# Sorting six sequences' rows by expert through DRAM in a one-core language model tower with 64 experts

## The chip, the cores and the metric

One core of a Trainium2 chip runs the whole computation in one launch. The metric is device microseconds, the median of several executions. Its five engines work in order, each through its own queue, and wait for one another on semaphores: TensorE (PE; its weight loads are PEld), VectorE (DVE), ScalarE (ACT), GpSimd (POOL) and SyncE (SP), which issues most DMAs.

## What is computed

Eight sequences of 512 tokens pass three parts. All data are fp32, D = 128.

```
e  = fine_embed[ids] ++ softmax(cluster_logits[ids] + b) @ coarse          # gather of 128 values per token
xn = rms_norm(layer_norm(e)); scores = xn qk xn^T * decay mask             # q, k, v, o folded into qk and vo
x2 = x1 + mem_mul * (scores @ xn vo)                                       # with a carried state per tile
h2 = e + x2 + op_mul * gelu(rms_norm(x2) @ read_mix + bias) @ write_w
x3 = layer_norm(h2)
p  = softmax(x3 @ router_w + b); the 6 largest of 64, normalised, are the gates
out = h2 + mean of 2 shared experts(x3) + sum over chosen experts: gate * (silu(x3 Wg) * (x3 Wu)) Wd
```

An expert has hidden size F = 64, and takes at most 768 tokens over all sequences, in token order; later ones are dropped.

## The kernel before, in words

Experts are taken in pairs, so that 2 x 64 hidden values fill 128 partitions: 32 routed pairs and one shared pair, `PAIRS` = 33. Every token goes through every pair, and the gate, zero where the expert was not chosen, is multiplied into the hidden values. Matrix products of the experts use fp32r (faster, less exact) three times each, on high and low parts: `gate_up` (L456 to L458) makes six products of 512 columns per pair, `down` (L443 to L445) three more, which lag by `LAG` = 4 pairs. Per pair ACT computes silu (L580) and copies the high part (L587), DVE multiplies by the up product (L828) and subtracts for the low part (L835), and POOL multiplies by the gate rows (L985). SP fetches those rows from `gates_dram`, broadcast over 64 partitions each (L278), into a ring of four.

The work of a sequence before its experts (call it the front part: embedding, attention, norms, router, gates) is written as steps placed at pair numbers by the tables `DVE_AT`, `PE_AT`, `ACT_AT`, `POOL_AT`. While sequence b runs its 33 pairs, the late steps of b + 1 and the early ones of b + 2 are issued in between, so one sequence's front part is spread over one to two sequences of pairs. Sequence 0's front part, and the split of the expert weights into high and low parts (ACT L614, DVE and POOL L257), run before the first pair. The token limit is kept by a running count (`taken`, L775, carried in `taken_end`), and the gates go to DRAM (L294).

## Time and profile before

| | |
|---|---|
| median of 3 runs | 775.56 us (775.4 to 778.88) |
| span of the profiled execution | 776.1 us, 0.5 us above that median |
| PE busy | 685.0 us, 88% |
| DVE busy | 636.5 us, 82% |
| POOL busy | 523.6 us, 67% |
| ACT busy | 430.9 us, 56% |
| moved by DMA | 80.20 MB, in 48862 packets |

The profile's times are those of one execution. Matmul records overlap, so the distance between two starts says what one costs, not its own length. "Idle before" names what ended the idle time in front of a group.

### The profile page before, as it was taken

To read this page: it belongs to the slowest core of one execution; us is meant where nothing else is said; L and a number is where in the kernel's file an instruction comes from. 1 tells how busy PE (TensorE), PEld (TensorE's weight loads), DVE (VectorE), ACT (ScalarE), POOL (GpSimd) and SP (SyncE) were. 2 spreads that over 40 slices of the span, in tenths; PEclk is the share of its full clock that TensorE was granted. 3 is DMA by queue.
4 is the path that set the end of the run, shared out by engine and by line. 5 is a ranking of instruction groups with operands and counts; after the bars stand their busy time and mean duration, and the time that the engine had idled before them with its cause. 6 is when DMAs were issued, how large, how long until landed. Compare 5 with 4: busy or idle time off the path is not lost.

```text
span 776.1 us, 11821 instructions
## 1 busy us (share of the span) xinstructions
PE 685.0 (88%) x3079; PEld 534.7 (69%) x3079; DVE 636.5 (82%) x1207; ACT 430.9 (56%) x745; POOL 523.6 (67%) x353
## 2 busy tenths in 40 slices
PE   4245899998998989997999989989899999999997
PEld 3234678766786677766777667867677688768885
DVE  4866778797898889898798988989888987897665
ACT  4333376643855557644666448555566456655553
POOL 5421667766676767767577677767677668768775
PEclk9976899998999999999999999999999999999999
DMA  5400423333333233224233333233333334425431
GB/s 210 156 31 0 129 86 106 107 95 93 94 101 112 91 99 122 97 77 123 81 115 102 96 92 114 98 108 99 98 110 98 93 115 121 118 78 144 139 128 58
DMA packets 48862, 80.20 MB, mean 103 GB/s; under 512 B 9504, under 2 KB 13728, under 8 KB 48800
## 3 DMA queue, kind: packets, MB, share of 16 engines
q1 hardware_dynamic: 47776, 77.44, 31.4%
q0 software_dynamic: 1024, 2.10, 1.2%
q8 instruction: 19, 0.31, 0.2%
q14 instruction: 43, 0.35, 0.1%
HBM read 76.35 MB, written 3.15 MB: 102 GB/s over the span
## 4 chain that ended last, share of the span: by engine, by line
DVE 25%; POOL 25%; issue 23%; PE 18%; ACT 3%; DMA 1%; POOLq 1%; SPq 1%; DVEq 0%; ACTq 0%
POOL hid L985 20%; DVE hid_lo L835 6%; DVE hid L828 5%; PE bank_u L456 2%; DVE xn L693 2%; PE bank_u L458 1%; PE bank_u L457 1%; POOL inv L966 1%; PE bank_g L456 1%; DVE turns L762 1%; PE bank_g L458 1%; PE bank_g L457 1%; PE bank_y L443 1%; PE bank_y L444 1%; PE bank_y L445 1%
## 5 line engine op out<-in xcount | busy, mean ns | idle before, releaser
L985 POOL TENSOR_TENSOR hid<-hid,gate_rows 128x512 f32<-128x512 f32 x256 | 412.8, 1623 | 177.7 <-DVE hid L828 174.5
L580 ACT ACTIVATE hid<-bank_g 128x512 f32<-128x512 f32 x264 | 157.6, 597 | 165.1 <-PE bank_g L458 159.8
L835 DVE TENSOR_TENSOR hid_lo<-hid,hid_hi 128x512 fp32r<-128x512 f32 x264 | 231.7, 878 | 17.7 <-ACT hid_hi L587 17.5
L828 DVE TENSOR_TENSOR hid<-hid,bank_u 128x512 f32<-128x512 f32 x264 | 179.0, 679 | 69.4 <-ACT hid L580 39.0
L587 ACT ACTIVATE hid_hi<-hid 128x512 fp32r<-128x512 f32 x264 | 165.9, 628 | 91.0 <-POOL hid L985 83.2
L456 PE MATMUL bank_g<-x_hi,gate_hi 128*128 128x512 f32 x264 | 115.7, 438 | 6.7 <-ACT hid L580 6.7
L456 PE MATMUL bank_u<-x_hi,up_hi 128*128 128x512 f32 x264 | 108.9, 412 | 3.0 <-DVE hid L828 2.7
L443 PE MATMUL bank_y<-hid_hi,down_hi 128*128 128x512 f32 x264 | 105.6, 400 | 3.1 <-ACT hid_hi L587 3.0
L457 PE MATMUL bank_g<-x_hi,gate_lo 128*128 128x512 f32 x264 | 105.7, 400 | 0.0
L444 PE MATMUL bank_y<-hid_hi,down_lo 128*128 128x512 f32 x264 | 105.6, 400 | 0.0
L458 PE MATMUL bank_g<-x_lo,gate_hi 128*128 128x512 f32 x264 | 105.4, 399 | 0.0
L458 PE MATMUL bank_u<-x_lo,up_hi 128*128 128x512 f32 x264 | 105.3, 399 | 0.0
L457 PE MATMUL bank_u<-x_hi,up_lo 128*128 128x512 f32 x264 | 105.2, 399 | 0.0
L445 PE MATMUL bank_y<-hid_lo,down_hi 128*128 128x512 f32 x264 | 104.9, 397 | 0.0
L456 PEld LDWEIGHTS bank_u<-x_hi,up_hi 128*128 128x128 f32 x264 | 50.5, 191 | 26.3 <-DVE hid L828 15.7
L443 PEld LDWEIGHTS bank_y<-hid_hi,down_hi 128*128 128x128 f32 x264 | 49.9, 189 | 20.6 <-ACT hid_hi L587 5.5
L456 PEld LDWEIGHTS bank_g<-x_hi,gate_hi 128*128 128x128 f32 x264 | 50.5, 191 | 19.6 <-ACT hid L580 9.6
L458 PEld LDWEIGHTS bank_u<-x_lo,up_hi 128*128 128x128 f32 x264 | 50.3, 191 | 12.2
L458 PEld LDWEIGHTS bank_g<-x_lo,gate_hi 128*128 128x128 f32 x264 | 50.4, 191 | 12.0
L445 PEld LDWEIGHTS bank_y<-hid_lo,down_hi 128*128 128x128 f32 x264 | 50.0, 189 | 12.1
L457 PEld LDWEIGHTS bank_u<-x_hi,up_lo 128*128 128x128 f32 x264 | 50.5, 191 | 10.2
L457 PEld LDWEIGHTS bank_g<-x_hi,gate_lo 128*128 128x128 f32 x264 | 50.6, 192 | 9.4 <-issue 1.7
(197 smaller groups left out, 836.9 us busy)
## 6 DMA issues: line engine op xcount, KB each, us to landing
gate_rows<-gates_dram SPq DMA_DIRECT2D x512, 128.0 KB, 2.9
hid<-gate_t_dram SPq DMA_DIRECT2D x3, 704.0 KB, 4.1
out_dram<-later SPq DMA_DIRECT2D x8, 256.0 KB, 3.0
gate_rows<-up_t_dram SPq DMA_DIRECT2D x2, 704.0 KB, 4.8
hid<-down_t_dram SPq DMA_DIRECT2D x2, 704.0 KB, 4.7
gates_dram<-gates_t SPq DMA_DIRECT2D x8, 128.0 KB, 2.3
later<-up_t_dram SPq DMA_DIRECT2D x1, 704.0 KB, 8.4
later<-down_t_dram SPq DMA_DIRECT2D x1, 704.0 KB, 6.2
```

What stands on the lines that cost most here:

```text
L443: pe.matmul(y[:, :], w_hi["down"][:, p, :], hid_hi[:, s, :], start=(p == 0), stop=False)
L444: pe.matmul(y[:, :], w_lo["down"][:, p, :], hid_hi[:, s, :], start=False, stop=False)
L445: pe.matmul(y[:, :], w_hi["down"][:, p, :], hid_lo[:, s, :], start=False, stop=(p == PAIRS - 1)).then_inc(sem("down_done"), 1)
L456: pe.matmul(o, w_hi[name][:, p, :], x3_hi[par][:, :], start=True, stop=False)
L457: pe.matmul(o, w_lo[name][:, p, :], x3_hi[par][:, :], start=False, stop=False)
L458: pe.matmul(o, w_hi[name][:, p, :], x3_lo[par][:, :], start=False, stop=True).then_inc(sem("pe_" + name), 1)
L580: act.activation(hid[:, slot(par, p), :], bank_g[(p + par) % 2][:, :], ACT.Silu).then_inc(sem("silu"), 1)
L587: act.activation(hid_hi[:, s, :], hid[:, s, :], ACT.Copy).then_inc(sem("hid_hi"), 1)
L693: last = dve.tensor_scalar(xn2[:, t, :], x2[:, t, :], inv2[:, t:t + 1], None, ALU.mult)
L828: dve.tensor_tensor(hid[:, s, :], hid[:, s, :], bank_u[(p + par) % 2][:, :], ALU.mult)\
L835: dve.tensor_tensor(hid_lo[:, s, :], hid[:, s, :], hid_hi[:, s, :].bitcast(F32), ALU.subtract)\
L985: pool.tensor_tensor(hid[:, s, :], hid[:, s, :], gate_rows[:, row, :], ALU.mult)\
```

## The change

Sequences 0 and 7 (`DENSE`) are treated as before: all 33 pairs, in place, but with one fp32 product where there were three fp32r ones, one PSUM bank each for gate (`bank_x`) and up (`bank_g`), and both multiplications on DVE. The other six (`SPARSE`) form two passes of three. In each:

- The running count starts at the expert's first row of a DRAM array `x_rows` (a stretch of 3200 rows per expert). `slots` holds, for each token, the rows of its six experts: the eight largest of a key per expert. POOL then scatters each tile of 128 tokens six times, each row holding the 128 values of x3 and the 64 gates (768 bytes).
- From the counts, `dve_lists` and `pe_lists` make a list of 136 tiles of 128 rows, each of one expert: offsets into the weights, gate column and DRAM row. The number is a fixed bound: 64 + (9216 - 64) / 128 = 135, rounded up to 34 steps of four tiles (`QUADS`), whatever the router does. A part of the list can be repeats.
- Each of the 34 steps loads four tiles (SP), transposes them, multiplies by gate and up weights side by side (128 columns), silu, times gate and up (DVE, 64 columns a tile), transposes, multiplies by the down weights, and ACT stores the four results to `y_rows`. The offsets are read from `lists` into registers, on SP, DVE and (twice) on PE.
- After a pass POOL fetches every token's six result rows (`y_slots`), and DVE sums them and adds them to h2.

The order is now written in half steps h, from -31 to 287, for all engines. A front part has 30 half steps; those of the eight sequences start at `START`. Sequence 0's pairs run from h = 0, two half steps each; pass one from h = 70, pass two from 138, sequence 7's pairs from 212. The shared experts of the six are computed apart (`shared_in`, `shared_out`). The norm's `hx` sum moves from POOL to DVE.

```diff
-CHUNKS = [(n, p0) for p0 in range(0, PAIRS, CHUNK) for n in ("gate", "up")] + \
-    [("down", p0) for p0 in range(0, PAIRS, CHUNK)]
+DENSE = (0, 7)
+PASSES = ((1, 2, 3), (4, 5, 6))
...
+ROW = D + EXPERTS
+ZEROS = P
+STRETCH = ZEROS + len(SPARSE) * SEQ
...
+START = (-30, -16, 0, 16, 32, 54, 76, 98)
+D_AT = {0: 0, 7: 212}
+E_AT = 70
+DOWN_LAG = 2
+LOAD_AHEAD = 6
...
+SCATTER_AT, SCATTERS_PER_HALF = 26, 1.5
+FETCH_AT = {0: E_AT + 2 * QUADS + 8, 1: E_AT + 2 * E_STEPS + 8}
+FETCHES_PER_HALF = 1.4
+COMBINE_LAG = 4
...
+        def sp_tiles(sp, g):
...
+            if g >= XT_RING:
+                sp.wait_ge(sem("hid"), g - XT_RING + 1)
+                sp.wait_ge(sem("pe_xt"), g - XT_RING + 1)
+            _, at = nc.values_load_multi_w_load_instructions(
+                lists[q][0:1, j, 3 * QUAD:4 * QUAD], engines=(ENG.SP,), min_val=0, max_val=EXPERTS * STRETCH - P)
+            for t in range(QUAD):
+                sp.dma_start(xt[:, g % XT_RING, t, :], x_rows[bass.ds(at[t], P), :])\
+                  .then_inc(sem(f"xt{g % XT_RING}"), 16)
...
-        def gate_up(pe, b, par, p):
...
-            for name, banks, freed in (("gate", bank_g, "silu"), ("up", bank_u, "up_used")):
-
-                wait(pe, freed, q - 1)
-                o = banks[ring][:, :]
-                pe.matmul(o, w_hi[name][:, p, :], x3_hi[par][:, :], start=True, stop=False)
-                pe.matmul(o, w_lo[name][:, p, :], x3_hi[par][:, :], start=False, stop=False)
-                pe.matmul(o, w_hi[name][:, p, :], x3_lo[par][:, :], start=False,
-                          stop=True).then_inc(sem("pe_" + name), 1)
+        def pe_dense(pe, d, b, p, half):
...
+                if p:
+                    pe.wait_ge(sem("silu"), q)
+                pe.matmul(bank_x[:, :], w_in[:, 0, p * P:p * P + P], x3_t(b)[:, :], start=True, stop=True)\
+                  .then_inc(sem("pe_gate"), 1)
+                if p:
+                    pe.wait_ge(sem("up_used"), q)
+                pe.matmul(bank_g[:, :], w_in[:, 1, p * P:p * P + P], x3_t(b)[:, :], start=True, stop=True)\
+                  .then_inc(sem("pe_up"), 1)
...
+        def pe_gate_up(pe, g):
+            q, j = divmod(g, QUADS)
+            _, at = nc.values_load_multi_w_load_instructions(
+                lists[q][0:1, j, 0:QUAD], engines=(ENG.PE,), min_val=P, max_val=P + (EXPERTS - 1) * F)
+            pe.wait_ge(sem("xT"), g + 1)
+            if g == 0:
+                pe.wait_ge(sem("up_used"), PAIRS)
+            else:
+                pe.wait_ge(sem("hid"), g)
+            for t in range(QUAD):
+                last = pe.matmul(bank_g[:, t * P:t * P + P], xT[:, g % 2, t * P:t * P + P], w_in[:, :, bass.ds(at[t], F)],
+                                 start=True, stop=True, skip_group_check=True)
+            last.then_inc(sem("pe_gu"), 1)
...
+        def dve_rows(dve, g):
+            q, j = divmod(g, QUADS)
+            _, at = nc.values_load_multi_w_load_instructions(
+                lists[q][0:1, j, 2 * QUAD:3 * QUAD], engines=(ENG.DVE,), min_val=D, max_val=ROW - 1)
+            dve.wait_ge(sem("sg"), g + 1)
+            wait(dve, "pe_hT", g - 1)
+            for t in range(QUAD):
+                last = dve.scalar_tensor_tensor(hid[:, g % 2, t * F:(t + 1) * F], sg[:, t, :],
+                                                xt[:, g % XT_RING, t, bass.ds(at[t], 1)], tiles(bank_g)[:, t, F:],
+                                                ALU.mult, ALU.mult)
+            last.then_inc(sem("hid"), 1)
+
+        def dve_combine(dve, m):
+            i, t = divmod(m, TILES)
+            b = SPARSE[i]
+            dve.wait_ge(sem(f"yg{m % YG_RING}"), 16 * TOP * (m // YG_RING + 1))
+            dve.tensor_reduce(ysum[:, m % 2, :], yg[:, m % YG_RING, :].rearrange("p (k d) -> p d k", d=D), AX.X, ALU.add)\
+               .then_inc(sem("y_sum"), 1)
...
+            dve.tensor_tensor(h2[b][:, t, :], h2[b][:, t, :], ysum[:, m % 2, :], ALU.add).then_inc(sem("combined"), 1)
...
+        def scatter(pool, b, i):
+            t, k = divmod(i, TOP)
...
+            pool.indirect_dma_start(x_rows[:, :],
+                                    bass.IndirectOffsetOnAxis(ap=slots[b][:, t * 8 + k:t * 8 + k + 1], axis=0),
+                                    xg[b % 2][:, t, :], None).then_inc(sem(f"scattered{b % 2}"), 16)
+
+        def fetch(pool, q, i):
...
+            if i == 0:
+                for r in range(Y_RING):
+                    pool.wait_ge(sem(f"y_stored{r}"), quad_rows(r, QUADS * (q + 1)))
...
+            if k == 0:
+                wait(pool, "y_sum", m - YG_RING + 1)
+            pool.indirect_dma_start(yg[:, m % YG_RING, k * D:(k + 1) * D], None, y_rows[q][:, :],
+                                    bass.IndirectOffsetOnAxis(ap=y_slots[b][:, t * 8 + k:t * 8 + k + 1], axis=0))\
+                .then_inc(sem(f"yg{m % YG_RING}"), 16)
```

In the order of instructions the change stands as follows. First PE's experts in place: one pair, before (PE's queue in the loop over sequences).

```order
L456 MATMUL bank_g<-x_hi,gate_hi 128x512
L457 MATMUL bank_g<-x_hi,gate_lo 128x512
L458 MATMUL bank_g<-x_lo,gate_hi 128x512
L456 MATMUL bank_u<-x_hi,up_hi 128x512
L457 MATMUL bank_u<-x_hi,up_lo 128x512
L458 MATMUL bank_u<-x_lo,up_hi 128x512
L443 MATMUL bank_y<-hid_hi,down_hi 128x512
L444 MATMUL bank_y<-hid_hi,down_lo 128x512
L445 MATMUL bank_y<-hid_lo,down_hi 128x512
```

The same engine with the change, at about pair 30 of sequence 0, beside the end of sequence 4's front part and the beginning of sequence 5's: L535, L539 and L548 are gate, up and down, the rest are front steps.

```order
L535 MATMUL bank_x<-x_t_dense,w_in 128x512
L539 MATMUL bank_g<-x_t_dense,w_in 128x512
L488 MATMUL bank_f<-w_dn,shared_hid 128x128 x4
L407 MATMUL bank_f<-xn_hi,qk_hi 128x512
L408 MATMUL bank_f<-xn_hi,qk_lo 128x512
L409 MATMUL bank_f<-xn_lo,qk_hi 128x512
L548 MATMUL bank_y<-y_sb,w_dn 128x512
```

Nine products per pair became three, and there is a group of front products between nearly all of them. Next the sparse steps on DVE, inside pass two: `bank_h` holds transposed hidden rows, L1053 is the product with silu and gate.

```order
L1174 COPY hT<-bank_h 64x256
L1048 TENSOR_LOAD lists
L1048 ISA x8
L1053 ISA
L1053 SCALAR_TENSOR_TENSOR hid<-sg,xt,bank_g 128x64
```

The last two rows come four times in a step. The kernel before has no load of registers on DVE; it stands here behind the copy of the step before. PE, in the same steps (L565 transposes the rows in, L578 is gate and up, L587 transposes the hidden rows):

```order
L565 MATMUL bank_x<-ident,xt 128x128 x4
L570 TENSOR_LOAD lists
L570 ISA x8
L578 ISA
L578 MATMUL bank_g<-w_in,xT 128x128
```
```order
L587 MATMUL bank_h<-ident,hid 128x128 x2
L592 TENSOR_LOAD lists
L592 ISA x8
L602 ISA
L602 MATMUL bank_y<-w_d,hT 128x128
```

Each of the two products comes four times behind its own load. Last POOL, while sequence 1 to 3 are scattered and, at the end of its queue, the fetches of both passes.

```order
L1195 DMA x_rows<-xg,slots 204800x192 x6
L1231 TENSOR_TENSOR inv<-var,neg_half 128x4
L1195 DMA x_rows<-xg,slots 204800x192 x4
L1220 TENSOR_TENSOR inv<-var,neg_half 128x8
L1195 DMA x_rows<-xg,slots 204800x192 x9
```
```order
L1195 DMA x_rows<-xg,slots 204800x192 x4
L1212 DMA yg<-y_rows,y_slots 128x128 x144
```

Where one gate product stood per pair (L985), POOL now issues indirect DMAs, with the powers of the norms between them.

## Rows read from the trace of the kernel before

**Rows 1.** The page, parts 1 and 4: busy time of each engine; chain by engine.
```profile
PE 685.0 (88%) x3079; PEld 534.7 (69%) x3079; DVE 636.5 (82%) x1207; ACT 430.9 (56%) x745; POOL 523.6 (67%) x353
...
DVE 25%; POOL 25%; issue 23%; PE 18%; ACT 3%; DMA 1%; POOLq 1%; SPq 1%; DVEq 0%; ACTq 0%
```

**Rows 2.** Stretches of the span; the columns are in the first line.
```profile
core 0: us, PE busy (x) PEld busy (x) DVE busy (x) ACT busy (x) POOL busy (x), PEclk, DMA share, GB/s
...
10.00:77.00 67.00, 30.57 (x114) 23.09 (x112) 48.45 (x116) 24.70 (x35) 21.99 (x13) 0.84 0.28 101
...
164.00:251.00 87.00, 80.12 (x359) 62.42 (x360) 72.66 (x140) 50.42 (x88) 60.32 (x41) 0.96 0.32 102
...
338.00:776.00 438.00, 409.60 (x1861) 320.08 (x1861) 364.63 (x656) 251.06 (x440) 313.02 (x203) 1.00 0.34 105
```

**Rows 3.** Groups by form: busy us, mean ns, idle before and releasers.
```profile
L985 POOL TENSOR_TENSOR hid<-hid,gate_rows 128x512 f32<-128x512 f32 x256 | 412.8, 1623 | 177.7 <-DVE hid L828 174.5 <-DMA gate_rows<-gates_dram 2.5
L835 DVE TENSOR_TENSOR hid_lo<-hid,hid_hi 128x512 fp32r<-128x512 f32 x264 | 231.7, 878 | 17.7 <-ACT hid_hi L587 17.5
L828 DVE TENSOR_TENSOR hid<-hid,bank_u 128x512 f32<-128x512 f32 x264 | 179.0, 679 | 69.4 <-ACT hid L580 39.0 <-PE bank_u L458 29.5
...
L580 ACT ACTIVATE hid<-bank_g 128x512 f32<-128x512 f32 x264 | 157.6, 597 | 165.1 <-PE bank_g L458 159.8 <-DVE hid_lo L835 2.1 <-issue 0.6
...
L682 DVE SCALAR_TENSOR_TENSOR turns<-turns,decay_cols,bank_f 128x128 f32<-128x128 f32 x16 | 5.6, 348 | 0.6
```

**Rows 4.** Timeline of PE: start us, us, instruction; one pair to the next.
```profile
310.64 0.39 PE L456 MATMUL bank_g<-x_hi,gate_hi 128*128 128x512 f32 x1
...
312.74 0.40 PE L456 MATMUL bank_g<-x_hi,gate_hi 128*128 128x512 f32 x1
```

**Rows 5.** Timeline of PE at three places: fp32 products and transposes.
```profile
297.19 1.02 PE L387 MATMUL bank_f<-xn_t,read_mix 128*128 128x512 f32 x2
...
298.28 0.39 PE L457 MATMUL bank_g<-x_hi,gate_lo 128*128 128x512 f32 x1
...
215.82 1.05 PE L393 MATMUL bank_f<-write_w,vals 128*128 128x128 f32 x8
216.63 0.48 PE L456 MATMUL bank_g<-x_hi,gate_hi 128*128 128x512 f32 x1
...
314.84 0.65 PE L399 MATMUL bank_f<-ident,xn 128*128 128x128 f32 x4
```

**Rows 6.** Timeline of DVE in the first sequence's front part.
```profile
22.57 3.90 DVE L644 TENSOR_SCALAR xn<-emb,mv,inv 128x128 f32<-128x128 f32 x4
...
26.39 1.61 DVE L257 TENSOR_TENSOR up_lo<-gate_rows,up_hi 128x1408 fp32r<-128x1408 f32 x1
...
33.65 4.03 DVE L650 TENSOR_SCALAR x<-emb,mv,inv 128x128 f32<-128x128 f32 x4
...
48.59 4.78 DVE L693 TENSOR_SCALAR xn<-shared,inv 128x128 f32<-128x128 f32 x4 [1.31 <-POOL inv L955]
...
63.02 1.12 DVE L716 TENSOR_SCALAR xn<-h,mv,inv 128x128 f32<-128x128 f32 x4 [0.80 <-POOL inv L961]
```

**Rows 7.** Timeline of POOL: two gathers.
```profile
4.86 0.94 POOL L945 DMA_INDIRECT emb<-table_dram,idx  x1 [0.30 <-issue]
...
6.11 0.94 POOL L945 DMA_INDIRECT emb<-table_dram,idx  x1 [0.30 <-issue]
```

**Rows 8.** Gate-row issues of SP (ns min/median/max), landing, and POOL's DMA queue.
```profile
L278 SPq DMA_DIRECT2D gate_rows<-gates_dram x512: 465/468/1425, 79.2 to 761.1; - x171
L278 SPq MOVE gate_rows<-gates_dram x256: 29/29/38, 165.7 to 521.4; - x128
L278 SPq FUSED_REGOPS  x254: 37/37/42, 165.7 to 521.3; - x127
...
q0 software_dynamic: 1024, 2.10, 1.2%
...
gate_rows<-gates_dram SPq DMA_DIRECT2D x512, 128.0 KB, 2.9
```

More of the change, by code:

```diff
@@ L43 @@
 SENTINEL = 2.0
-RING = 6
-GATE_RING = 4
-LAG = 4
-SPLIT_LAG = 2
-GATHER_AT = (1, 2, 3, 4)
-DVE_AT = dict(xn=0, xn_lo=2, x1=5, xn_dec=5, y_lo=4, scores=6, state=6, x2=8, result=10, logits=9, xn2=11, exp_sum=12,
-              h=15, bn1=16, h2=17, bn3=17, mv1=18, x3=19, x3_lo=21, router=24, prob=26, top=27, chosen=28, gates=29,
-              taken=31)
-PE_AT = dict(xn_t=1, y=3, z_scores=5, state=6, mem=7, out=8, exp_t=11, xn2_t=12, vals=13, coarse=14, op=16, x3_t=20,
-             router=23, gates_t=30)
@@ new lines @@
+TILE_BOUND = EXPERTS + (ROWS_OF_PASS - EXPERTS) // P
+QUADS = (TILE_BOUND + QUAD - 1) // QUAD
+LIST = QUADS * QUAD
+MAX_TILES = len(PASSES[0]) * SEQ // P
+XT_RING, Y_RING, YG_RING = 4, 3, 3
+GATE_RING, HID_RING = 3, 3
+START = (-30, -16, 0, 16, 32, 54, 76, 98)
[3 more added lines that the diff above has]
+LOAD_AHEAD = 6
+E_STEPS = len(PASSES) * QUADS
+H_FIRST, H_LAST = START[0] - 1, D_AT[7] + 2 * (PAIRS + DOWN_LAG) + 6
+DVE_AT = dict(logits=0, exp_sum=2, h=3, xn=5, xn_lo=6, xn_dec=6, x1=7, y_lo=7, scores=8, state=9, x2=10, hx=11, xn2=13,
+              h2=16, x3=18, router=20, prob=22, chosen=23, taken=24, slots=25, shared_up=27, shared_add=29)
@@ L542, in act_late @@
                 act.wait_ge(sem("pe_z_scores"), b + 1)
[L543 to L547 removed]
+                for j in range(2):
+                    act.activation(z[:, 2 * j:2 * j + 2, :], z_scores(par, j)[:, :, 0, :], ACT.Copy).then_inc(sem("z"), 1)
@@ L838, in dve_out @@
[L838 to L856 removed]
+            if k == DVE_AT["taken"]:
+                dve_taken(dve, b, f1)
@@ new lines, in _ @@
+                for d, b in enumerate(DENSE):
+                    if h == D_AT[b] + 2 * (PAIRS + DOWN_LAG) + 2:
+                        dve.wait_ge(sem("pe_out"), d + 1)
+                        dve.tensor_tensor(h2[b][:, :, :], tiles(bank_y), h2[b][:, :, :], ALU.add).then_inc(sem("result"), 1)
+                now = step_e(h)
+                if now:
+                    s, half = now
+                    if half == 0 and 0 <= s - 2 < E_STEPS:
+                        g = s - 2
+                        dve.wait_ge(sem("pe_hT"), g + 1)
+                        wait(dve, "pe_ey", g - 1)
+                        dve.tensor_copy(hT[:, g % 2, 1, :], bank_h[F:, 0:2 * P]).then_inc(sem("hT_odd"), 1)
+                    if half == 0 and 0 <= s - 1 < E_STEPS:
+                        dve_rows(dve, s - 1)
```

1302 lines of the change are left out of this document (759 added, 543 removed).

## The prediction

> **What bounds the kernel now.** I read the engines' totals first, then busy time by stretch, the costliest groups, and last the order of single matmuls. PE is busy for 88% of the span and DVE for 82%, while the chain that ended last is spread over DVE, POOL, issue and PE [rows 1]. The stretches say more [rows 2]: 67 us (10 to 77) go to the first sequence's front part, with PE busy for 31 us only; from there every sequence takes 87 us, with PE busy for 80 and DVE for 73. So after 77 us TensorE sets the pace. One expert pair is nine fp32r products of 512 columns; the gate product of one pair starts at 310.64 and that of the next at 312.74, so a pair costs 2.10 us [rows 4], and 33 pairs 69 of the 87 us. The reader should see that ScalarE, POOL and the gate-row transfers have slack, and that DVE has little.
>
> **What the change removes.** All eight sequences now pay 33 pairs; afterwards two do. Also gone: the weight splits, the hi/lo splits of hidden rows (264 x 0.88 us of DVE), and POOL's gate product (256 x 1.62 us) [rows 3]. POOL's arithmetic also held DVE up: three groups of four small DVE operations took 3.90, 4.03 and 4.78 us in the first front where another such group took 1.12 [rows 6].
>
> **Prices.** An fp32 product of 512 columns: the two records begin at 297.19, and the product after the next starts at 298.28; less the 0.23 us (2.10 / 9) of the product between, that is 0.86 us [rows 5]. An fp32 product of 128 columns: eight records (four products) from 215.82 to the next start at 216.63, 0.20 each [rows 5]. Four transposes take 0.65 us at most, about 0.4 in a stream [rows 5]. A dense pair is thus 3 x 0.86 = 2.6 us of PE where it was 2.1: one fp32 product costs more than two fp32r ones but less than four. On DVE it is two products of 0.68, 1.36 us [rows 3]; the old second operation's 0.88 included waits for POOL. A front part costs DVE 72.7 - 33 x (0.68 + 0.88) = 21 us [rows 2, 3]; with the slot keys, the second gate pass and the shared expert's two operations I take 24 for a sorted sequence. It costs PE 80.1 - 69.3 = 11, with the new products 13. As a chain it took 67 us (10 to 77); less the 9.3 us above what three normal groups need, and five weight splits of 1.6 us [rows 6], some 49 us, over 25 of the new half steps: 2.0 us each.
>
> **Unseen prices.** The register load (one from `lists` per sparse step on DVE and on SP, two on PE) appears nowhere. Its lower end is a register operation's 0.03 to 0.04 us, since a register could fill as fast as it is moved; its upper end is a whole DMA round trip, 2.9 us from issue to landing [rows 8]. I take 1.2 us, nearest to a POOL indirect issue of 0.94 to 1.25, which also makes a sequencer fetch and compute [rows 7]. For eight bounds checks and four address operations I take 0.4 us at 0.03 to 0.04 each [rows 8]. The gate product of 64 columns on DVE (four per step): below the 0.35 us of the 128-column form from PSUM [rows 3], above nothing; 0.25. Scatter and fetch: the gathers start 1.25 us apart (4.86, 6.11) [rows 7], and I take that for all 288 new ones. [...]
>
> **Stage by stage** (half steps h of the new order).
> A, until h = 0. Ten us of loading, 14 halves with one front at 2.0, 16 with two at 2.5: 10 + 28 + 40 = **78 us**. Before, this stage ended at 77 [rows 2]. Dropping the weight splits is eaten by letting front 1 run through its 17th step first.
> B, h 0 to 70: first sequence dense, fronts 2 to 5 beside it. DVE: 3.9 fronts x 24 + 5 for the tile lists + 33 x 1.36 = 144 us, 2.1 per half; PE: 33 x 2.6 + 3.9 x 13 = 136. Neither the floors nor the 2.0 chain can all be met, because every engine is in order and heavy steps meet: with fronts 16 halves apart, layer norm meets the new logits, top-8 meets xn_lo, the gates meet y_lo, and the counts meet the scores. These four halves hold about 18.5 us of DVE; the other twelve go at the chain's 2.0. (18.5 + 24)/16 = 2.7. 70 x 2.7 = **189 us**. POOL's 72 scatters (90 us) lie beside this.
> C, pass one, 34 steps, fronts 5 (second half), 6 and 7 beside. A sparse step is a loop: PE gate/up of step s (4 x 0.20), its hidden transposes and signal (0.4), DVE copy (0.35), DVE register load and checks (1.6), four products (1.0), then gate/up of s + 1: 4.15 us. DVE holds 2.95 of that. The fronts add 72/34 = 2.1 to the same in-order queue, 5.05 in all, and fill most of the hole; I add 0.45 for waits: 34 x 5.5 = **187 us**.
> D, pass two, no front left after a few steps. The loop alone, 4.15, raised to 4.5 because PE's sequencer has two loads with checks (3.2) and some 50 matrix instructions to send in the same time: 34 x 4.5 = **153 us**. The first pass's fetches (72 x 1.25 = 90) and sums lie in DVE's hole.
> E, drain of three steps, **9 us**, then the last sequence dense. Alone it would be 33 x 2.6 + 8 = 94. But the 72 fetches of pass two start only now, need 90 us on POOL, and DVE waits in order for each fourth of them: 94 us with landing until the last sum, which stands at half 56 of the dense stage; 14 halves at 1.3 remain, then 8 us of tail. **120 us**.
> Sum: 78 + 189 + 187 + 153 + 9 + 120 = **736 us**, against the profiled execution's own span of 776.1, which is 0.5 above the median of the runs, 775.56; I leave it uncorrected. In short, eight stages of 87 us, bound by PE arithmetic, turn into about 660 us bound by DVE and by sequencer latency. The arithmetic shrinks far more than the time does.
>
> **The clock.** [...] A pure sparse step keeps PE busy for 2.3 of 4.5 us, 51%. I charge nothing: the mean of 0.84 would add 0.15 us to the gate/up part, 10 us in all. [...]
>
> **Rivals.**
> R1, faster, 630 us. The queues overlap better than I think: halves in B at DVE's own 2.2 (154), C at 4.9 (167), D at 3.6 because loads overlap the hidden transposes (122), fetches not held up by a slow start, E at 100: 78 + 154 + 167 + 122 + 9 + 100. For it: from 164 to 251 PE is busy for 92% of the stretch although the same fronts run beside it [rows 2]. Against: there a front had 33 pairs of slack, now 8.
> R2, slower, 811 us. The register load on DVE sits inside the loop of every sparse step. At 2.3 us it adds 1.1 x 68 = 75 us. It decides from (776 - 736)/68 = 0.6 us more, that is from 1.8 us per load. For: a DMA round trip is 2.9 us; against: nothing has to be written and signalled.
> R3, slower, 796 us. DMA becomes the bound. In D a step moves 393 KB of tiles, 262 KB of results and 180 KB of fetches, 186 GB/s, where 105 GB/s took a share of 0.34 [rows 2]: 0.60 at the same price. If rows of 512 to 768 bytes cost double, a step needs 5.4 us, +0.9 x 68. Against: the gathers' 4096 rows of 512 bytes took 1.2% of sixteen engines' span, 36 ns each [rows 8].
> R4: B and C go worse, 3.2 per half and 6.5 per step, 805 us.
>
> **How the numbers follow.** Forecast 0.48, R1 0.18, R2 0.20, R3 0.07, R4 0.07. About 0.5% (4 us) is what a measurement of this kernel can tell from no change. The forecast's own range, 690 to 790, has 0.38 below 772; with R1 and a little of R2 to R4 faster has 0.57, same 0.06, slower 0.37. The range 640 to 850 leaves out half of R1 and the far ends of R2 to R4. Since both signs are likely, the likeliest case's own range matters: 690 to 790.
>
> **What would show it.** Right: DVE between a hidden-row copy and the next one spends about 1.2 us in which nothing is busy (the load); pure sparse steps 4.5 us apart; first dense stage 175 to 205 us long with PE under 75% busy; POOL issues spaced 1.25 us and DVE waiting for `yg` in the last stage. Wrong: sparse steps under 3.8 or above 5.3 us, tiles arriving after PE asks for them (waits of PE for `xt`), a granted clock near 0.5 through pass two, or a front that takes far more than 16 halves' time. Gates or slots cannot shorten the work: 34 steps per pass run whatever the router picks.

## The result, and the profile after

The changed kernel takes 823.57 us (median of 4 runs, 821.62 to 824.75) against 776.96 (775.40 to 778.88) for the kernel before, a ratio of 1.0587 with a 95% interval of 1.0549 to 1.0625: 6% slower, where 736 us and 5% faster was forecast. The profiled execution has a span of 823.0 us.

The page of the changed kernel: totals, granted clock in 40 slices, chain, and the groups that carry the new work (line, engine, operation, names | busy us, mean ns | idle before them and its releasers).

```profile
PE 615.1 (75%) x2709; PEld 424.9 (52%) x2709; DVE 427.3 (52%) x1308; ACT 280.5 (34%) x543; POOL 354.7 (43%) x361
...
PEclk9999799899999968668667987989897866899898
...
PE 43%; DVE 21%; POOL 13%; issue 13%; DVEq 4%; ACT 3%; DMA 1%; POOLq 0%; SPq 0%; ACTq 0%
...
L1212 POOL DMA_INDIRECT yg<-y_rows,y_slots x144 | 139.9, 972 | 191.4 <-DMA y_rows<-y_sb 128.5
...
L578 PE MATMUL bank_g<-w_in,xT 128*128 x544 | 104.2, 352 | 33.3 <-DVE hid L1053 19.0
L602 PE MATMUL bank_y<-w_d,hT 64*128 x544 | 95.9, 327 | 34.8 <-DVE hT L1174 26.6
...
L1053 DVE SCALAR_TENSOR_TENSOR hid<-sg,xt,bank_g 128x64 f32<-128x64 f32 x272 | 58.6, 275 | 86.7 <-issue 86.5
L1174 DVE COPY hT<-bank_h 64x256 f32<-64x256 f32 x68 | 29.0, 426 | 123.7 <-PE bank_h L587 123.0
```

Against the same parts of before [rows 1], every engine lost work (DVE 636.5 to 427.3 us, PE 685.0 to 615.1), and none is near its limit: the time went into waits between engines. DVE stood idle 86.7 us ahead of L1053, the gating of the rows, with nothing named but "issue" (1.27 us a step, over 68 steps), and 123.7 us ahead of L1174 for PE's transposes, while PE waited for both of these. Two engines that wait for each other are a loop, not a bottleneck.

The span by stage. The bounds are starts of PE instructions: the first dense product (L535, 88.1), the row transposes (L565) of step 0 (283.7), of step 27, the first with no front part beside it (489.4), of step 34 (pass two, 523.9) and of the last, step 67 (685.6).

```profile
core 0: us, PE busy (x) PEld busy (x) DVE busy (x) ACT busy (x) POOL busy (x), PEclk, DMA share, GB/s
0.00:88.10 88.10, 47.01 (x171) 36.34 (x172) 41.64 (x153) 20.08 (x43) 19.72 (x28) 0.96 0.62 196
88.10:283.70 195.60, 157.60 (x609) 85.66 (x609) 146.47 (x450) 78.89 (x137) 123.04 (x116) 0.97 0.29 96
283.70:489.40 205.70, 146.54 (x795) 123.58 (x792) 98.82 (x376) 80.97 (x158) 72.04 (x73) 0.74 0.37 108
489.40:523.90 34.50, 27.26 (x156) 22.78 (x155) 9.21 (x37) 13.18 (x28) 0.00 (x0) 0.80 0.46 131
523.90:685.60 161.70, 125.49 (x727) 104.98 (x726) 63.12 (x193) 61.61 (x132) 68.65 (x72) 0.83 0.62 169
685.60:823.00 137.40, 111.21 (x261) 51.58 (x260) 68.04 (x103) 25.74 (x45) 71.26 (x72) 0.87 0.42 115
```

| stage | forecast | measured |
|---|---|---|
| A, until the first dense product | 78 | 88 |
| B, sequence 0 dense, fronts 2 to 5 | 189 | 196 |
| C, pass one (34 steps) | 187 | 240 |
| D, drain and E, pass two to the end | 282 | 299 |

Of the 87 us that the forecast lacks, 53 lie in C, and there in its first 27 steps: 7.6 us each where 5.5 was forecast. The last seven took 4.9 each, and the 33 steps from 34 to 67 also 4.9, against a forecast of 4.5.

One such step on the timeline (start us, us, instruction [idle before <-releaser]), here at full clock:

```profile
649.98 0.85 DVE L1053 SCALAR_TENSOR_TENSOR hid<-sg,xt,bank_g 128x64 f32<-128x64 f32 x4 [1.27 <-issue]
...
651.10 1.15 PE L578 MATMUL bank_g<-w_in,xT 128*128 x8 [0.55 <-DVE hid L1053]
...
652.09 0.38 PE L587 MATMUL bank_h<-ident,hid 128*128 128x128 f32 x2
...
652.51 0.42 DVE L1174 COPY hT<-bank_h 64x256 f32<-64x256 f32 x1 [1.68 <-PE bank_h L587]
...
653.50 1.15 PE L602 MATMUL bank_y<-w_d,hT 64*128 x8 [1.03 <-DVE hT L1174]
...
654.21 0.86 DVE L1053 SCALAR_TENSOR_TENSOR hid<-sg,xt,bank_g 128x64 f32<-128x64 f32 x4 [1.27 <-issue]
```

This is the loop that the forecast described: gating, gate and up products, hidden transposes, copy, load, next gating: 4.23 us from 649.98 to 654.21 (forecast 4.15). The steps alone take longer than this loop, 4.64 on average in the 19 of them in which the granted clock was 1.00; the first question below shows that most of the rest is PE's own queue. What the 1.27 and 1.03 us hold, the two sequencers show (ns min/median/max):

```profile
L570 PEldq FUSED_REGOPS  x272: 146/148/165, 285.7 to 690.2; - x136
L570 PEldq SEQ_ASSERT  x272: 18/18/24, 285.9 to 690.5; - x136
L570 PEldq TENSOR_LOAD <-lists x68: 327/333/594, 285.1 to 689.0; - x68
...
L1048 DVEq FUSED_REGOPS  x272: 183/186/211, 291.6 to 695.1; - x136
L1048 DVEq SEQ_ASSERT  x272: 23/23/41, 291.9 to 695.3; - x136
L1048 DVEq TENSOR_LOAD <-lists x68: 339/342/598, 291.0 to 693.9; - x68
```

A load of four words takes 0.33 to 0.34 us. The range check that goes with every word is the pair FUSED_REGOPS and SEQ_ASSERT of these lines; it takes 0.166 us on PE (148 + 18 ns) and 0.209 on DVE, so the four cost 0.66 and 0.84, two thirds of the whole: 1.0 us on PE, twice a step, 1.18 on DVE.

### The profile page after: what moved, and what is told of

Its sections match the earlier page's. It is cut to its first block, busy times and chain, and to the rows that moved or that the text cites. A ratio compares the mean times of both kernels' runs of the same rounds, so it can differ in the third digit from the quotient of the medians.

```text
span 823.0 us, 13195 instructions
## 1 busy us (share of the span) xinstructions
PE 615.1 (75%) x2709; PEld 424.9 (52%) x2709; DVE 427.3 (52%) x1308; ACT 280.5 (34%) x543; POOL 354.7 (43%) x361
## 3 DMA queue, kind: packets, MB, share of 16 engines
q0 software_dynamic: 12544, 25.71, 10.7%
## 4 chain that ended last, share of the span: by engine, by line
PE 43%; DVE 21%; POOL 13%; issue 13%; DVEq 4%; ACT 3%; DMA 1%; POOLq 0%; SPq 0%; ACTq 0%
PE bank_g L578 11%; POOL yg L1212 8%; PE bank_y L602 6%; PE bank_x L565 4%; DVEq L1048 4%; POOL x_rows L1195 3%; DVE hid L1053 2%; DVE hT L1174 2%; PE bank_h L587 2%; PE bank_x L535 2%; PE bank_g L539 2%; PE bank_f L432 2%; PE bank_y L548 1%; PE bank_f L396 1%; PE bank_f L435 1%
## 5 line engine op out<-in xcount | busy, mean ns | idle before, releaser
L1212 POOL DMA_INDIRECT yg<-y_rows,y_slots x144 | 139.9, 972 | 191.4 <-DMA y_rows<-y_sb 128.5
L1195 POOL DMA_INDIRECT x_rows<-xg,slots x144 | 145.7, 1012 | 65.8 <-issue 41.7
L578 PE MATMUL bank_g<-w_in,xT 128*128 x544 | 104.2, 352 | 33.3 <-DVE hid L1053 19.0
L602 PE MATMUL bank_y<-w_d,hT 64*128 x544 | 95.9, 327 | 34.8 <-DVE hT L1174 26.6
L578 PEld LDWEIGHTS bank_g<-w_in,xT 128*128 128x128 f32 x544 | 91.7, 255 | 46.2 <-issue 46.1
L602 PEld LDWEIGHTS bank_y<-w_d,hT 64*128 64x128 f32 x544 | 81.2, 226 | 52.8 <-issue 52.8
L1053 DVE SCALAR_TENSOR_TENSOR hid<-sg,xt,bank_g 128x64 f32<-128x64 f32 x272 | 58.6, 275 | 86.7 <-issue 86.5
L1174 DVE COPY hT<-bank_h 64x256 f32<-64x256 f32 x68 | 29.0, 426 | 123.7 <-PE bank_h L587 123.0
L539 PE MATMUL bank_g<-x_t_dense,w_in 128*128 128x512 f32 x132 | 71.9, 627 | 17.0 <-DVE xt L1151 17.0
L535 PE MATMUL bank_x<-x_t_dense,w_in 128*128 128x512 f32 x132 | 74.7, 650 | 0.0
L539 PEld LDWEIGHTS bank_g<-x_t_dense,w_in 128*128 128x128 f32 x132 | 26.5, 207 | 56.1 <-issue 29.7
L565 PE MATMUL bank_x<-ident,xt 128*128 128x128 f32 x272 | 54.2, 333 | 0.3 <-ACT xT L761 0.3
L766 ACT ACTIVATE sg<-bank_g 128x256 f32<-128x256 f32 x68 | 26.1, 383 | 83.0 <-PE bank_g L578 82.9
L749 ACT ACTIVATE xt<-bank_x 128x512 f32<-128x512 f32 x33 | 19.7, 597 | 90.9 <-PE bank_x L535 84.4
L565 PEld LDWEIGHTS bank_x<-ident,xt 128*128 128x128 f32 x272 | 37.3, 169 | 8.1 <-issue 3.5
L548 PE MATMUL bank_y<-xt,w_dn 128*128 128x512 f32 x66 | 36.3, 638 | 0.0
```

What stands on the lines that cost most here:

```text
L535: pe.matmul(bank_x[:, :], w_in[:, 0, p * P:p * P + P], x3_t(b)[:, :], start=True, stop=True)\
L539: pe.matmul(bank_g[:, :], w_in[:, 1, p * P:p * P + P], x3_t(b)[:, :], start=True, stop=True)\
L548: pe.matmul(bank_y[:, :], w_dn[:, p, :], hid_d[b][:, p % HID_RING, :], start=(p == 0), stop=(p == PAIRS - 1)).then_inc(sem("down_done"), 1)
L565: last = pe.transpose(bank_x[:, t * P:t * P + P], xt[:, r, t, 0:D], ident[:, :])
L578: last = pe.matmul(bank_g[:, t * P:t * P + P], xT[:, g % 2, t * P:t * P + P], w_in[:, :, bass.ds(at[t], F)], start=True, stop=True, skip_g ...
L602: last = pe.matmul(bank_y[:, t * P:t * P + P], hT[:, g % 2, t % 2, (t // 2) * P:(t // 2 + 1) * P], w_d64[:, bass.ds(at[t], P)], start=True ...
```

## The experiments

Times of the kernel before, beside these runs, had medians of 777.29 to 778.42 us; the ratios are to those. For each kernel I read the same three stretches as above: steps 0 to 27 (beside fronts), 27 to 67 (alone), and from step 67 to the end. These stretches are those of one profiled execution each, and differences of a few us between them mean little: the last one took 137.4 us in the changed kernel and 132.4 to 135.4 in five kernels whose edits hardly touch that stage (e1, e2, e3, e5, e13).

| kernel | median us | ratio, 95% interval | 0-27 | 27-67 | rest |
|---|---|---|---|---|---|
| changed | 823.57 | 1.0549 to 1.0625 | 205.7 | 196.3 | 137.4 |
| e1_pe_nocheck | 801.39 | 1.0262 to 1.0315 | 191.3 | 195.5 | 133.6 |
| e2_dve_nocheck | 786.04 | 1.0080 to 1.0135 | 176.8 | 188.9 | 132.4 |
| e3_dve_load_first | 788.80 | 1.0117 to 1.0151 | 181.3 | 191.5 | 133.8 |
| e4_both | 708.95 | 0.9072 to 0.9128 | 159.9 | 135.5 | 127.0 |
| e9_nocheck_all | 709.50 | 0.9089 to 0.9178 | 160.8 | 134.4 | 128.7 |
| e6_filler | 819.30 | 1.0511 to 1.0549 | 204.0 | 194.6 | 132.9 |
| e8_both_filler | 730.38 | 0.9347 to 0.9418 | 168.2 | 146.1 | 129.1 |
| e10_one_load | 710.92 | 0.9104 to 0.9231 | 158.5 | 135.3 | 126.5 |
| e5_late_rows | 898.17 | 1.1513 to 1.1598 | 138.4 | 201.9 | 135.4 |
| e13_copy_later | 781.94 | 1.0037 to 1.0084 | 170.1 | 190.3 | 132.4 |
| e14_copy_later_nocheck | 698.82 | 0.8968 to 0.9067 | 146.3 | 134.0 | 128.5 |
| e16_swap_later_nocheck | 788.84 | 1.0118 to 1.0183 | 234.8 | 140.5 | 129.4 |
| e7_no_fetch | 801.52 | 1.0247 to 1.0334 | 207.0 | 199.3 | 111.5 |
| e11_rate | 693.55 | 0.8886 to 0.8970 | 159.8 | 132.2 | 114.2 |
| e12_best | 699.51 | 0.8932 to 0.9029 | 160.1 | 136.3 | 114.1 |
| e15_all | 688.35 | 0.8815 to 0.8888 | 149.9 | 137.2 | 114.7 |
| e17_checks_kept | 769.60 | 0.9875 to 0.9912 | 170.5 | 189.8 | 119.7 |

**First question: what do load and checks cost, and on which engine?** Theory T1: PE's queue is the loop. T2: the loop runs through DVE. The range checks are left out with an argument of the load call; the computation is the same.

```diff
 e1, at both of PE's loads; e2, at DVE's load
-  ..., min_val=..., max_val=...)
+  ..., min_val=..., max_val=..., skip_runtime_bounds_check_because="...")
 e3 (e4: this, and no checks on PE, DVE and SP)
+                    at = dve_load(s - 1) if half == 0 and 0 <= s - 1 < E_STEPS else None
                     if half == 0 and 0 <= s - 2 < E_STEPS:
                         g = s - 2
                         dve.wait_ge(sem("pe_hT"), g + 1)
```

> The four range checks behind each of PE's two register loads per sparse step are left out; nothing else changes. Theory T1 (PE's own queue is the loop of a sparse step: rows in, load, gate/up, hidden transposes, load, down; 4.6 us at full clock): a step without fronts falls from 4.6 to about 4.15, where the loop through DVE takes over, and the time by 30 to 45 us, to about 785. Theory T2 (the loop runs through DVE's copy, load and four products, as the prediction had it): no change, 823 within 5.

> The four range checks behind DVE's register load are left out, 0.6 us of DVE's queue per sparse step. T1 (PE's queue is the loop): within 8 us of the changed kernel's 823. T2 (the loop through DVE): 0.6 x 68 = 41 us less, 782.

> DVE's register load and checks stand before its wait for the hidden transposes instead of behind it, so 1.3 us leave the loop through DVE (copy, load, products) and fall into its idle time. T1: within 10 us of 823. T2: 1.3 x 68 = 88 us less, 735.

> No range checks on PE, DVE and SP, and DVE's load first. T1: PE's queue becomes 4.6 - 1.3 = 3.3 us at full clock and DVE's loop 2.5, so the step without fronts goes to 3.4 to 3.8 and the time falls by 68 x 1.0 or more, to 730 to 755. T2: as e3, 735, with e1 unchanged. If the clock falls because PE's work gets no denser, less.

Neither theory holds alone, and 709 lies below every forecast for e4. Each single edit gains 22 to 38 us, about three quarters of it beside the fronts; steps alone hardly move (4.91 to 4.89, 4.72 and 4.79 us). Both together gain 115, of which 61 in the steps alone: 3.39 us each. What PE waited for ahead of its two products changes hands, and goes only when both queues are short. In order: e1, e2, e4.

```profile
L578 PE MATMUL bank_g<-w_in,xT 128*128 x544 | 106.0, 357 | 45.3 <-DVE hid L1053 42.3 <-ACT xT L761 2.8 <-issue 0.3
L602 PE MATMUL bank_y<-w_d,hT 64*128 x544 | 96.9, 330 | 1.1 <-ACT y_sb L778 0.9 <-issue 0.2
```

```profile
L578 PE MATMUL bank_g<-w_in,xT 128*128 x544 | 106.1, 357 | 19.9 <-issue 12.4 <-ACT xT L761 6.3 <-DVE hid L1053 0.8
L602 PE MATMUL bank_y<-w_d,hT 64*128 x544 | 98.7, 334 | 28.8 <-DVE hT L1174 23.9 <-ACT hT L772 3.1 <-ACT y_sb L778 0.9
```

```profile
L578 PE MATMUL bank_g<-w_in,xT 128*128 x544 | 84.7, 304 | 6.5 <-DVE hid L1055 5.5 <-issue 0.9
L602 PE MATMUL bank_y<-w_d,hT 64*128 x544 | 81.9, 293 | 4.3 <-issue 1.7 <-ACT y_sb L778 1.1 <-ACT hT L772 0.5
```

With PE's checks gone (e1), all of the wait is for DVE's gating; with DVE's gone (e2), it is "issue" and the wait for the copy, behind which PE's own second load and checks stand. So a step has two rounds of similar length, one on each queue, and the longer one counts.

That is not all that kept the single edits small in the steps alone. The granted clock over steps 27 to 67 fell too: 0.82 in the changed kernel, 0.76, 0.76 and 0.75 in e1, e2 and e3, 0.94 in e4. At the same clock more is seen. Six steps in a row at full clock (33 to 38) and two at a granted clock of 0.54 (63, 64) in the changed kernel, and six at full clock (45 to 50) in e1, in the columns of the windows above:

```profile
518.96:546.93 27.97, 18.66 (x133) 15.14 (x132) 8.07 (x32) 10.98 (x24) 1.69 (x2) 1.00 0.52 145
663.83:674.85 11.02, 10.47 (x46) 8.90 (x45) 4.09 (x13) 3.90 (x8) 0.00 (x0) 0.54 0.46 129
```

```profile
566.39:592.45 26.06, 18.48 (x133) 15.13 (x132) 11.05 (x34) 11.60 (x25) 15.41 (x18) 1.00 0.74 198
```

At full clock a step took 4.66 us, and 4.34 without PE's checks, on the way to the 4.15 to 4.23 of DVE's loop, as T1 has it; with the clock at 0.54 it took 5.51, and PE was busy for 95% of it, so there PE's own work set the pace. The lower clock of e1 hides in its mean what the shorter queue had given.

To see whether the place of DVE's load matters at all once it is short, e9 drops the checks everywhere and leaves the load where it was:

> No range checks on any queue, but DVE's register load back in its place between the copy of the transposed hidden rows and the gating (the kernel of 708.95 us has it ahead). Single edits gave -22 (PE's checks), -37 (DVE's checks), -35 (DVE's load ahead), together -115. Theory T3 (two queues take turns as the bound: a step costs the longer of PE's round and DVE's round, so either edit on DVE alone stops at PE's round of 4.5 us and PE's alone at DVE's): without checks DVE's load is 0.35 us, PE's products bound the step at 3.1 anyway, so only 0 to 0.35 x 68 us is lost: 709 to 733. Rival (moving the load is worth 35 us whatever the checks cost, since it takes the load off the way from PE to DVE to PE): 744.

709.5 us, the same as e4: T3 holds, and the rival falls. The checks alone are worth 114 us. (SP's are among them in e4 and e9 and have no run of their own; in the changed kernel PE never waited for the tiles that SP loads, so they were hardly on its path.) e10 takes one load of eight words on PE in place of two of four (`lists[q][0:1, j, 0:2 * QUAD]`, the down offsets kept until two steps later):

> The kernel of 708.95 us with one register load of eight words on PE in each step in place of two of four. In its trace PE idles 0.15 us (issue) ahead of the gate and up products and 0.35 to 0.37 us (issue) ahead of the down products in a step of 3.09. Theory L1 (a load costs 0.33 us whatever it brings in): 68 x 0.35 = 24 us less, 685. Theory L2 (it costs by the register, 0.08 us each): the time is the same, 709, and the idle moves ahead of the gate and up products.

No gain (710.92, in four runs from 707.14 to 718.03, against 708.95). The load of eight took 0.59 us at the median where four took 0.33, so most of it goes by the word (0.065 us each and some 0.07 once). L2 is right about the time; the idle time ahead of the down products went from 4.3 to 1.1 us as L1 has it, and the wait for DVE's gating rose from 5.5 to 8.6. PE's round is not all that is left of the step. The steps at full clock show the place of DVE's load too: 3.36 us on average in e9 (all 40), where it stands inside the loop, and 3.17 in e4 (35 of 40), whose other five, in which the clock fell, took 4.9.

**Second question: is it the clock?** It was 0.74 beside the fronts and 0.83 in pass two (0.82 over steps 27 to 67), lower than the 0.96 to 1.00 of the dense stages before [rows 2]. Two extra products per step keep PE at work during its waits:

```diff
+        def filler(pe, bank):
+            pe.matmul(bank[:, 0:2 * P], ident[:, :], w_in[:, 0, 0:2 * P], start=True, stop=True, skip_group_check=True)
...
             wait(pe, "hT_odd", g)
+            filler(pe, bank_h)
+            pe.wait_ge(sem("hid"), g + 1)
...
+            filler(pe, bank_y)
             pe.wait_ge(sem("hT_even"), g + 1)
```

> The changed kernel with two extra fp32 products of 256 columns in every step of rows, into a bank that is overwritten afterwards: one ahead of the wait for the gated hidden rows, one behind PE's second register load ahead of the wait for the transposed hidden rows. They read nothing that the fronts or steps write. Theory C (the granted clock, 0.73 to 0.76 in the stretches 283 to 386, 386 to 491 and 600 to 704, is a price of its own): the fillers lie in idle time and raise it; steps alone go from 4.9 to 4.5 (45 steps, -18), the steps beside fronts lose up to a quarter of the 150 us that PE is busy in 283 to 494, of which half is on the path (-18): 785 to 795. Theory Q (the steps wait in the queues for register loads, checks and for each other, and the clock only follows): no change where the fillers hide, 820 to 826, and up to 68 x 0.86 = 58 us more where they don't, 880.

> The kernel without range checks and with DVE's load ahead of its wait (708.95 us), with the same two fillers in each step. There a step alone takes 3.0 us at a granted clock of 1.00 in a stretch of 460 to 494 us, and PE is busy 33.3 of 34 us, so it has no idle time for the fillers; beside fronts the clock is 0.83 to 0.84. Theory C (clock a price of its own beside fronts): at best 12 us less there, and 45 steps x 0.86 x (1.0 to 0.5 hidden) = 20 to 39 more in the steps alone: 717 to 735. Theory Q: 747 if all fillers stand on the path.

The fillers did raise the clock (third from the end in the columns of the windows above):

```profile
285.30:489.40 204.10, 155.51 (x893) 126.24 (x891) 99.78 (x380) 82.19 (x158) 71.85 (x72) 0.86 0.38 109
489.40:683.90 194.50, 166.74 (x1041) 126.24 (x1040) 71.62 (x224) 77.80 (x160) 68.55 (x72) 1.00 0.60 164
```

The steps alone went from 4.91 to 4.86 us with the clock at 1.00 instead of 0.82, those beside fronts from 7.6 to 7.6 with 0.86 instead of 0.74: 819.3 us in all, next to theory Q's 820. Steps of the changed kernel that ran at full clock took 4.64, so a filled step carries about 0.2 us of the fillers' own work, 14 us over 68 steps if it is the same beside fronts; what the fillers gave back of the clock is then some 18 us (14 + 4), an estimate, and not the 53 that are missing. It is not the whole price of the clock. In the steps alone that price is at most 196.3 - 40 x 4.64 = 11 us, as if every step had run at full clock. Beside the fronts the fillers gave back about half of what was missing (0.74 to 0.86), no run had a full clock there, and how much of the 205.7 us the clock costs stays open. e8 lost 21 us. That lies within theory C's range, but not for its reason: the stretch beside fronts, which should have gained up to 12 us, lost 8.

**Third question: why do the fronts cost so much?** Put 56 halves later, the rows' steps run alone:

```diff
-D_AT = {0: 0, 7: 212}
-E_AT = 70
+D_AT = {0: 0, 7: 268}
+E_AT = 126
```

> The changed kernel with the sorted rows' steps and the last dense sequence moved 56 halves later (E_AT 126, D_AT[7] 268), so that no front part stands beside a step of rows. In the changed kernel the first 27 steps, which share their halves with fronts 5 to 7, took 210 us (283.7 to 494.1), 7.8 each, against 4.7 to 5.0 for a step alone; so the fronts added 83 us there. The 61 front halves that are left alone cost 2.0 each by the chain of my forecast, 122 us. Theory S (front work and row steps in one half mostly add up, because every queue works through both in order): the total moves little, 823 + (122 - 83) = 862 at most, and 823 if a lone front half costs 1.4. Theory O (the fronts were hidden beside the steps, as my forecast took it with 5.5 a step, and the steps were long for another reason such as the clock): the steps stay at 6 to 7 us also when alone, or the total rises by 100 and more, to 920.

The windows of that kernel: fronts 5 to 7 alone, steps 0 to 27 alone, steps 27 to 67, the rest.

```profile
283.70:416.70 133.00, 59.48 (x245) 43.43 (x244) 66.97 (x248) 25.50 (x51) 72.26 (x74) 0.64 0.17 54
416.70:555.00 138.30, 117.60 (x559) 99.61 (x557) 34.38 (x128) 49.80 (x102) 0.00 (x0) 0.64 0.44 120
555.00:756.90 201.90, 165.93 (x882) 140.13 (x881) 72.04 (x227) 75.72 (x160) 68.55 (x72) 0.75 0.58 158
756.90:892.30 135.40, 110.80 (x261) 50.78 (x260) 68.47 (x104) 25.77 (x45) 70.30 (x72) 0.88 0.42 117
```

The result, 898 us, lies between the theories. The fronts alone take 133 us (the 56 halves from 70 to 125, 2.4 each; the expectation had counted 61), the 27 steps alone 138; together they took 206. So about half of the fronts' time was hidden and 67 us showed. Without checks (e9) it is 160.8 - 27 x 3.36 = 70 us: checks and steps shrink, the fronts' 70 stay. Part of what holds them is seen in the changed kernel between 308 and 319 us, rows of PE and DVE:

```profile
308.96 0.42 DVE L945 TENSOR_TENSOR chosen_gates<-chosen_gates 128x256 f32<-128x256 f32 x1
...
309.44 1.11 PE L466 MATMUL bank_f<-ident,chosen_gates 128*128 128x128 f32 x4 [3.12 <-DVE chosen_gates L945]
...
313.99 0.18 DVE L803 RECIPROCAL soft<-soft 128x4 f32<-128x4 f32 x1
...
314.27 1.10 PE L396 MATMUL bank_f<-coarse_sb,z 64*128 64x64 f32 x8
...
315.30 0.44 PE L587 MATMUL bank_h<-ident,hid 128*128 128x128 f32 x2
...
315.78 0.43 DVE L1174 COPY hT<-bank_h 64x256 f32<-64x256 f32 x1 [1.61 <-PE bank_h L587]
...
317.48 0.86 DVE L1053 SCALAR_TENSOR_TENSOR hid<-sg,xt,bank_g 128x64 f32<-128x64 f32 x4 [1.28 <-issue]
318.25 0.62 DVE L954 MAX8 key<-bank_f 128x8 f32<-128x64 f32 x4
318.58 1.15 PE L578 MATMUL bank_g<-w_in,xT 128*128 x8 [1.17 <-DVE hid L1053]
```

DVE's copy L1174 stands in the even half of a step, PE's transposes L587 that it waits for in the odd half after it, behind PE's front work of the even half (L396 at 314.27). So DVE cannot begin its front work of the odd half (L954) until PE has ended that of the even half, and PE's next front work waits for DVE: the two take turns. One digit undoes this:

```diff
-                    if half == 0 and 0 <= s - 2 < E_STEPS:
+                    if half == 1 and 0 <= s - 2 < E_STEPS:
                         g = s - 2
                         dve.wait_ge(sem("pe_hT"), g + 1)
```

> The changed kernel with one number changed: DVE copies its part of the transposed hidden rows in the odd half of a step, the one in which PE transposes them, and no longer in the even half before. As it stands DVE's copy in half h waits for PE's transposes of half h + 1, so DVE's front work of half h + 1 stands behind PE's of half h (in the trace DVE ends a front piece at 313.99 and its next one begins at 318.25, behind L1174 at 315.78 that waited for PE's L587 at 315.30). Theory H (this handshake is why the fronts added 73 us to the first 27 steps): between 20 and 50 of the 73 go, the steps alone stay at PE's round of 4.5 to 4.9: 773 to 803. Rival R (a front's chain of single results, 49 us long, adds up whatever the place of the copy): 815 to 825.

> The same edit on the kernel without range checks (709.5 us). Its first 27 steps took 160.8 us, 70 more than 27 of its steps alone at 3.36. H: 660 to 690. R: 705 to 712.

On the changed kernel it gives 41.6 us, 36 of them in steps 0 to 27, 6 in the steps alone: theory H. Without checks it gives only 10.7, with 14.5 in steps 0 to 27; 698.8 lies between H's 660 to 690 and R's 705 to 712, so neither holds there. That the handshake costs most where load and checks stand inside it fits both, but is argued. Some 56 us that the fronts add there (146.3 - 27 x 3.35) remain, and no run took them apart further. A front's own chain of single results is one candidate. The traces show another that no forecast had: beside the fronts ScalarE changes its function table between the steps' SiLU (L766) and the fronts' functions (L671, L698, L709), 15 loads of 1.28 us each in steps 0 to 27 (19 us of ACT, in the changed kernel and in e9 and e14 alike), where e5 has one in the same steps alone and seven in its fronts alone. How much of it lies on the path is not shown.

e16 then puts the step's work ahead of the fronts' on ACT and DVE as well:

> The kernel of e14 with the work of the step of rows placed ahead of the front work in each half on ACT and DVE too, as it is on PE. H in its wider form (order in the queues): a few us either way of e14, since PE's order then matches, -10 to +5. R: no change, 705 to 712.

Both theories missed by far: 90 us slower than e14, 88 of them in steps 0 to 27. DVE now waits in every even half for PE's gate and up products of that half and ScalarE's SiLU before it may do front work. Its rows of the same place as above (L1055 is the gating, L749 the line of `sg` in this kernel):

```profile
310.83 1.11 PE L466 MATMUL bank_f<-ident,chosen_gates 128*128 128x128 f32 x4 [6.78 <-DVE chosen_gates L945]
...
316.13 0.85 DVE L1055 SCALAR_TENSOR_TENSOR hid<-sg,xt,bank_g 128x64 f32<-128x64 f32 x4 [5.35 <-ACT sg L749]
```

PE waited 6.78 us for the front's gates, where it had been 4.63 in e14, and DVE 5.35 us for ScalarE's `sg`. Over the whole span DVE's wait for `sg` went from 68.9 us in e14 to 147.4. The order of work on two in-order queues was worth nearly as much (90 us) as the range checks (114).

**Fourth question: what paces the last stage?** e7 leaves out five of six fetches of pass two (the sums for sequences 4 to 6 are then incomplete); e11 spreads them.

```diff
 e7
+            if q and k:
+                return
 e11 (on e4)
-FETCHES_PER_HALF = 1.4
+FETCHES_PER_HALF = {0: 1.4, 1: 1.0}
```

> The changed kernel, in whose second pass five of each six indirect fetches of result rows are left out, so the results of sequences 4 to 6 are not summed up rightly; everything on DVE stays. Theory P (the last stage, 119 us beside the dense sequence 7, is paced by POOL's fetches, as I forecast: 72 of 1.25 us and waits for DVE's sums): the stage falls to 33 pairs x 2.6 + 9 = 95 us, total 799. Theory V (DVE's sums of 1.47 us and PE's own clock pace it): 815 to 823.

> The kernel of 708.95 us with the second pass's fetches spread at 1.0 per half instead of 1.4 (each is 1.25 to 1.27 us on POOL), beside the dense sequence 7, whose last stage takes 118 us for 70 halves: 1.69 us per half, which is 1.4 x 1.25 = 1.75 less a little. Theory P (in each half the other engines wait for the sums of what POOL has fetched, so the halves run at POOL's rate per half): at 1.0 a half they run at 1.3, PE's own pace, and POOL's 72 x 1.27 = 91 us still have to be paid: stage of 100, total 691. Rival V (it is the 24 sums and additions on DVE, or the number of fetches in all, that cost): 705 to 715.

In order the last stretch of e7 and of e11:

```profile
690.20:801.70 111.50, 101.23 (x261) 48.77 (x260) 67.78 (x104) 25.66 (x45) 11.41 (x12) 0.92 0.36 106
```

```profile
576.20:690.40 114.20, 96.53 (x261) 45.03 (x260) 69.52 (x106) 25.55 (x45) 70.36 (x72) 0.93 0.50 141
```

Without five sixths of the fetches the stretch falls from 137.4 to 111.5, with all of them at the slower rate from 127.0 to 114.2, although POOL is as busy as before (70.36 us): theory P both times, with a last stage somewhat longer than the 100 us that it gave e11. The fetches were issued in halves faster than POOL could do them (one starts 1.25 us after the other, e.g. at 713.52 and 714.77 in the changed kernel), and the other engines' halves ran at POOL's rate.

**Combinations.**

> Both of the last two edits together. Different stages, so they add: with L1 and P 667; with L1 alone 685, with P alone 691.

> The kernel of e14 with the second pass's fetches at 1.0 per half, which alone gave -15.4 us (708.95 to 693.55) in the last stage. Another stage, so the two add: 15 below e14, 645 to 675 by H, 692 by R.

> The changed kernel with all its range checks, with two edits: DVE's copy in the odd half (-41.7 us alone, of the 823.57) and the second pass's fetches at 1.0 per half (-15.4 alone, on the kernel without checks). Different stages, so they should add: 781.94 - 13 to 15 = 767 to 769, 1% under the kernel before. Rival: with steps still at 4.8 us the dense stage begins as before and gains the same, but the first pass's fetches and the second's now touch and cost it again: 775 to 780.

e12 shows no gain from the single load (699.5, 6 above e11, and above every figure of its expectation). e15 is the fastest: 688.35 us, ratio 0.885. It is 10.5 us below e14 where 15 were expected, above H's 645 to 675, and 5 below e11. e17 keeps every check and, with the digit and the fetch rate alone, comes to 769.6 us, 1.1% under the kernel before (ratio 0.9875 to 0.9912): as the sum said. It is the one kernel here that does all of the changed kernel's work, checks included, and is not slower than the kernel before.

## Why the prediction was wrong

**Direction and size.** 736 us forecast, 823.57 measured; 0.37 had been given to slower. The number lies within the range, beyond the likeliest case's own (690 to 790).

**C, 187 against 240: the step that failed.** "The fronts add 72/34 = 2.1 to the same in-order queue, 5.05 in all, and fill most of the hole; I add 0.45 for waits". The busy time was right, the filling was not: DVE's hole is inside a round trip to PE, and the copy's wait for the next half's transposes keeps front work out of it. Measured, the fronts add 67 us to 27 steps (e5), 2.5 per step, where the forecast had them add 1.35 to its loop of 4.15; moving the copy (e13) took off 36 us there. The rest of the 53 us is the step itself, 4.9 alone where the loop had been 4.15 (next paragraph). R4, 6.5 per step, came nearest to the mean of 7.1, with a chance of only 0.07.

**D, 4.5 against 4.9.** The reason given, PE's sequencer with its two loads, was right: without PE's checks a step at full clock went from 4.66 to 4.34 (e1), toward the loop's 4.15. Of the excess over 33 steps, 13 us, steps at full clock (4.64) leave about 5 to the two queues and up to 8 to the granted clock, which "I charge nothing" left out.

**The load.** "1.2 us" and "0.4 us" for the checks sum to 1.6; measured are 1.18 on DVE (0.34 and 0.84) and 1.0 on PE. The sum was a quarter high against the 1.27 us of idle time, the parts the wrong way round: a check's register operations took 148 and 186 ns, where the 29 to 37 ns of [rows 8] had been the price. That made the checks look like nothing to question; taking them away is worth 114 us, more than the whole distance to the kernel before. A register of this list, which lies in SBUF, took 0.08 (0.33 / 4). R2 (811 us, a load of 2.3) came out near the time for a reason that did not occur.

**The clock.** "I charge nothing" stood beside 10 us for a mean of 0.84, the granted clock of the stretch 10 to 77 [rows 2]. No row of before shows what a step costs at another clock; measured in the changed kernel, it took 5.51 us at 0.54 and 4.66 at 1.00, 0.85 more. What failed was to charge nothing: up to 11 us in the steps alone, and an unknown part beside the fronts (some 18 in all for what the fillers gave back). The granted clock was 0.74 beside the fronts, with PE busy for 71% of the stretch, 0.83 in pass two, with 78%, and 1.00 in the steps alone with fillers, with 86%. But six steps in a row ran at 1.00 with PE busy for 67%, and two at 0.54 with 95%: how the clock follows from PE's idle time is not shown. By its records PE never idled for more than 1.15 us at a time in steps 27 to 67, and "a granted clock near 0.5 through pass two" did not come.

**A, 78 against 88.** It had 2.0 for a half with one front and 2.5 with two. The 56 halves of fronts alone in e5, 40 with one and 16 with two, would be 120 us by these prices and took 133, 11% more. The same 11% of A's 68 us would be 7 of the 10, an estimate; the other 3 no run took apart.

**B, 189 against 196, and the last stage.** The times held: fronts that meet cost 2.8 per half (forecast 2.7), and from step 67 the measured 137 stand against 134 (a step of 4.5, 9 and 120); POOL's pacing is confirmed by e7 and e11. One term and one sign of B did not hold: PE was busy for 158 us, 81% of the stretch, where 136 and under 75% were forecast; DVE's 146 (forecast 144) did. R3, DMA as the bound, did not come: the share was 0.62 in pass two. In e4, without checks, it reached 0.86, and PE then waited for `xt` for 3.8 us in all.

**R1**, the queues overlapping better, is what the kernels without checks show from step 27: 3.4 us a step, under its 3.6.
